# Eight token transfers per chunk of a recurrence, begun by GpSimd on its own queue instead of by SyncE

## The reference, cut to what matters

```python
x_proj = x @ W_in
xs, z = jnp.split(x_proj, 2, axis=-1)
delta = xs @ W_delta
Bv = xs @ W_B
Cv = xs @ W_C
deltaA = jnp.exp(jnp.einsum('bld,dn->bldn', delta, A))
deltaB = jnp.einsum('bld,bln->bldn', delta, Bv)

def step(state, inp):
    dA_i, dB_i, x_i, C_i = inp
    state = dA_i * state + dB_i * x_i[:, None, :]
    y = jnp.einsum('bdn,bn->bd', state, C_i)
    return (state, y)
```

## Time and profile before

| | before |
|---|---|
| median of three runs | 7372.27 us (7366.63 to 7378.81) |
| the profiled execution: its time / span | 7362.99 us / 7361.1 us |
| mean granted TensorE clock | 0.970 |
| recurrence, first to last scan | 2277.07 to 7018 us |
| VectorE busy | 6478.1 us (88%) |
| TensorE busy | 6408.9 us (87%) |
| GpSimd busy | 2747.4 us (37%) |
| transfers of tokens | 2048 of 16 KB and 128 of 4 KB, all issued by SyncE |

### The profile page before, as it was taken

The page is one execution under the profiler, slowest core; times in us unless marked ns, Lnnn a source line. Parts: engine busy times, 40 slices in busy tenths (PEclk is TensorE's granted clock), DMA queues, the critical chain, the costliest instruction groups (busy, mean ns, idle before and its releaser), DMA issues. The chain is left out here.

```text
span 7361.1 us, 173597 instructions
## 1 busy us (share of the span) xinstructions
PE 6408.9 (87%) x52385; PEld 3911.8 (53%) x52385; DVE 6478.1 (88%) x4166; ACT 4524.9 (61%) x9561; POOL 2747.4 (37%) x1996
## 2 busy tenths in 40 slices
PE   8999999999786888888888888888888888888867
PEld 3555547555344555555555555555555555555535
DVE  7888878888557999999999999999999999999962
ACT  7888868888464555555555555555555555555541
POOL 5555445555234333333333333333333333333300
PEclk9999999999898999999999999999999999999985
DMA  6666666666693111111111111111111111111154
GB/s 144 153 156 154 155 144 155 154 154 155 199 321 83 27 27 27 28 27 27 28 26 27 28 27 28 27 27 28 27 26 28 26 29 27 27 27 28 27 171 113
DMA packets 918664, 569.20 MB, mean 77 GB/s; under 512 B 710606, under 2 KB 819054, under 8 KB 917870
## 3 DMA queue, kind: packets, MB, share of 16 engines
q1 hardware_dynamic: 917885, 560.17, 32.1%
HBM read 161.99 MB, written 125.17 MB: 39 GB/s over the span
## 5 line engine op out<-in xcount | busy, mean ns | idle before, releaser
L1059 DVE TENSOR_TENSOR_SCAN states<-decay,enter_ps 128x1024 f32<-128x1024 f32 x2048 | 4468.2, 2262 | 172.3 <-ACT enter_ps L965 167.2
L876 PE MATMUL enter_ps<-s_steps,s_tokens 128*128 128x128 bf16 (+1 forms) x16384 | 2139.3, 311 | 625.6 <-DVE states L1059 514.5
L876 PEld LDWEIGHTS enter_ps<-s_steps,s_tokens 128*128 128x128 bf16 (+1 forms) x16384 | 1596.2, 130 | 1738.5 <-DVE states L1059 1569.4
L950 ACT ACTIVATE decay<-rate_ps 128x504 f32<-128x504 f32 x4096 | 2196.3, 588 | 98.0 <-PE rate_ps L854 23.8
L1016 POOL TENSOR_SCALAR s_wide<-s_rates,mask 128x512 bf16<-128x512 bf16 (+1 forms) x1088 | 1619.5, 1506 | 488.3 <-DMA s_rates<-rates_dram 353.8
L965 ACT COPY enter_ps<-states 128x16 f32<-128x16 f32 x1920 | 363.1, 189 | 1655.4 <-PE enter_ps L876 1649.6
L854 PE MATMUL rate_ps<-s_wide,s_decays 128*128 128x256 bf16 x8192 | 1330.9, 285 | 34.4 <-POOL s_wide L1016 33.7
L243 POOL TENSOR_TENSOR entered<-gates 128x512 f32<-128x512 f32 x512 | 900.9, 1760 | 888.8 <-ACT gates L203 888.8
L900 PE MATMUL y_ps<-states,spread 128*32 128x512 f32 x8320 | 1117.9, 609 | 0.4 <-issue 0.4
L1022 POOL COPY spread<-s_readout 128x64 f32<-128x64 f32 (+1 forms) x272 | 63.6, 234 | 2565.4 <-PE y_ps L900 2009.9
L854 PEld LDWEIGHTS rate_ps<-s_wide,s_decays 128*128 128x128 bf16 x8192 | 897.5, 119 | 95.8 <-issue 36.8
(11 more groups left out here) (154 smaller groups left out, 2310.4 us busy)
## 6 DMA issues: line engine op xcount, KB each, us to landing
rows<-feat SPq DMA_DIRECT2D x1024, 132.0 KB, 2.4
rows<-feat SPq DMA_DIRECT2D x512, 128.0 KB, 2.4
s_steps<-steps_dram SPq DMA_DIRECT2D x4096, 8.0 KB
rows<-feat SPq DMA_DIRECT2D x512, 127.8 KB, 2.4
s_rates<-rates_dram SPq DMA_DIRECT2D x256, 128.0 KB, 2.6
s_tokens<-tokens_dram SPq DMA_DIRECT2D x2048, 16.0 KB
rates_dram<-parts SPq DMA_DIRECT2D x32, 768.0 KB, 4.6
steps_dram<-steps SPq DMA_DIRECT2D x32, 768.0 KB, 8.0
```

Of the source, the lines that this page charges most:

```text
L876: mm = pe.matmul(out.rearrange("p h l -> p l h"), tokens[s][0:n * TERMS, k, :], steps[s][0:n * TERMS, k, 0:n, d:d + half], start=True, sto ...
L950: act.activation(decay[i][:, HEADS // 2 * h:HEADS // 2 * (h + 1), 1:], rate_ps[h][:, :, 0:n], ACT.Exp).then_inc(decay_ready, 1)
L1059: dve.tensor_tensor_scan(out, factor, term, 0.0, ALU.mult, ALU.add).then_inc(scanned, 1)
```

## The change

The eight transfers of tokens go from SyncE's `load` to GpSimd's `chunk`, between the widening and the wait for the readout. With them goes a copy of the wait for `enter_ready`; SyncE keeps its own for the steps. The tokens get semaphores of their own (`tokens_in`), and TensorE waits for both kinds. Sizes, addresses and the number of transfers stay the same.

```diff
+        tokens_in = [ctx.enter_context(nc.semaphore(f"scan_tokens_in{s}")) for s in range(SETS)]
...
-        LOADS = BLOCK + TERMS
...
                 sp.wait_ge(enter_ready, units_to(b, before(c) + 1))
                 sp.sem_inc(passed, 1)
-                for e in range(TERMS):
-                    a = STATE * (e // SPLITS)
-                    src = tokens_dram[bass.ds(b, 1), t0:t0 + n, a:a + STATE].rearrange("b (k t) n -> (b t) k n", t=BLOCK)
-                    sp.dma_start(tokens[s][e::TERMS, :, :], src).then_inc(enter_in[s], DMA)
                 for t in range(BLOCK):
...
-                    pe.wait_ge(enter_in[s], SCAN0 + (turn_of(b, c) + 1) * LOADS * DMA)
+                    pe.wait_ge(enter_in[s], SCAN0 + (turn_of(b, c) + 1) * BLOCK * DMA)
+                    pe.wait_ge(tokens_in[s], (turn_of(b, c) + 1) * TERMS * DMA)
...
                 w.then_inc(widened[s], 1)
+                pool.wait_ge(enter_ready, units_to(b, before(c) + 1))
+                pool.sem_inc(passed, 1)
+                for e in range(TERMS):
+                    a = STATE * (e // SPLITS)
+                    src = tokens_dram[bass.ds(b, 1), FULL * c:FULL * c + n, a:a + STATE].rearrange(
+                        "b (k t) n -> (b t) k n", t=BLOCK)
+                    pool.dma_start(tokens[s][e::TERMS, :, :], src).then_inc(tokens_in[s], DMA)
                 pool.wait_ge(readout_in[s], SCAN0 + (turn + 1) * DMA)
```

## The result

| | before | after |
|---|---|---|
| median (runs) | 7375.54 us (four, 7366.63 to 7379.01) | 7266.84 us (four, 7257.00 to 7271.46) |
| profiled execution: time / span | 7362.99 / 7361.1 us | 7257.00 / 7255.2 us |
| mean granted TensorE clock | 0.970 | 0.975 |

The ratio of the times is 0.9853, 95% interval 0.9836 to 0.9870: **faster by 1.5%, some 109 us**. The forecast was 7330 with a range from 7275 to 7510. The direction was right, the size was not.

The account below looks back on a forecast made before the run. Bound by VectorE's scans, and 14 times by SyncE's issuing. Holes -79 and -4, late chunk 0' +35 and first chunk +6 sum to -42 us: 7321 profiled, 7330 us on the median, range 7275 to 7510.

Parts of the forecast that it names:

- SyncE's issuing bounds the recurrence at 3': Before chunk 3 of the next batch, 14 times, scans wait for steps that SyncE issues 6 us late.
- 79 and 4 us of holes: VectorE's idle time before chunk 3' and right behind (79), and before chunks 1' and 2' (4); all predicted to go.
- the three loads 1', 2', 3': SyncE's loads between a batch end and the late steps; relieving them gives 16 us against a lateness of 6.
- The price x: GpSimd's time for one token transfer, taken as 1.0 us; the forecast sum is zero at 1.17.
- the chain: GpSimd's serial work at the batch end: eight issues, spread, loop end, widening, eight issues, landing; on time up to 0.86 us each.
- the +35: Chunk 0', first of the next batch, late 15 times by 16 - 13.7 us at 1.0 us per transfer.
- the formula: Chunk 0' late by 16x - 13.7 us, 15 times; first chunk later by 8x - 1.8; x is GpSimd's time per transfer.
- First chunk, +6: Before the very first scan: eight token issues on GpSimd make it 8 - 1.8 us later.
- The 17 us of second holes left: Second and third holes behind chunk 0' in some batches, 17 us in all, predicted to stay.
- The rival that counted them (7277): GpSimd nearly as quick as SyncE, x up to 0.86, second holes gone too: 7277 us; chance 0.22.
- Inside the batch nothing changes, and VectorE does not lock GpSimd out: Within a batch, 15.9 of 17.46 us needed, cost 0; rival of VectorE locking out GpSimd: 11500 us, chance 0.02.
- A draw or slower, 0.42 together: Draw: 0' takes what 3' gives, 7372 us, chance 0.13. Slower: GpSimd's serial chain bounds, 7505 to some 8400, chance 0.29.

Follow-up runs that it names:

- The runs with three chunks each: The change, but GpSimd begins tokens only of chunks 1, 2, 3 (0.9888), 15, 16, 0 (0.9859) or 8, 9, 10 (0.9992); ratios to the kernel before.
- the tokens on ScalarE one unit sooner: Kernel before with tokens begun by ScalarE, two transfers in unit 0, one in units 1 to 6, none in unit 7: 0.9896 of the kernel before.
- the run with chunks 1, 2, 3: The change with GpSimd beginning the tokens only of chunks 1, 2 and 3 of each batch, SyncE the others: 0.9888 of the kernel before.
- doubled: The change with every token transfer issued a second time by GpSimd, into a spare tile: 7321.54 us, 0.9928 of the kernel before.
- tripled: The change with two extra token transfers by GpSimd for each, 24 issues per chunk: 7766 us, 1.0536 of the kernel before.

## Why the prediction was wrong where it was

1. *SyncE's issuing bounds the recurrence at 3'; taking eight issues off each load ends that.* Right: I had added up 79 and 4 us of holes in the trace of before, and all of them went (79.3 and 3.8). The runs with three chunks each bear it out: relief near the batch end works, relief in mid-batch doesn't. The view that it takes the three loads 1', 2', 3' was right but too narrow. Relief ahead of 0' does as much.

2. ***The price x*: the step that failed.** I took 1.0 us and bounded it by 0.69 from below and 1.8 from above. The chip shows 0.51, half the forecast's value and below the lower bound. Two faults lie in it. The upper bound carried over a ratio from elementwise work (1760 against 678 ns) to an instruction that moves no elements. And the lower bound, SyncE's 0.69, held 0.13 us of register work between two issues; on GpSimd eight issues follow one another in 4.1 us with no gap between them. Even the 0.557 us of SyncE's instruction alone is more than GpSimd's 0.508. A bound "from below" that is another engine's price is no bound. With 0.51 the chain gives 16 x 0.51 = 8.2 against 13.7: no lateness at 0', and the +35 vanish. The rest of the chain was sized too short, which did not matter here: the formula would leave 5.5 us to spare at 0', and the trace has 2.8. GpSimd stood 1.44 us ahead of the issues for chunk 16, where I had nothing, and 2.86 us at its loop's end for 1.8, and the landing takes 2.0 us for 1.5.

3. *First chunk, +6.* The same fault and nothing else. With x = 0.51 the formula gives 4.1 - 1.8 = +2.3; the hole grew by 2.5.

4. *The 17 us of second holes left, because "they hang on the restart of TensorE after a pause".* Wrong in its conclusion, and the second fault in size. I had read the last link of the chain and not its first. The trace of before had the row (TensorE's timeline, batch end at 3454 us):

```profile
3456.11 1.03 PE L876 MATMUL enter_ps<-s_steps,s_tokens 128*128 128x128 bf16 x8 [1.34 <-DMA s_steps<-steps_dram]
3456.94 0.64 PE L854 MATMUL rate_ps<-s_wide,s_decays 128*128 128x256 bf16 x4
3460.45 1.62 PE L876 MATMUL enter_ps<-s_steps,s_tokens 128*128 128x128 bf16 x8 [2.87 <-DVE states L1059]
```

TensorE waited for the steps of 0' first, and was slower after that. At the five batch ends of this trace where it waited 1.28 us or more for them, the two later holes add up to 15.7 of the 17.4 us. The lateness had a cause, and it was SyncE. These holes went with the change, stayed where only 1, 2, 3 were relieved, and came back where GpSimd was made late. The link that I did name is not empty, though: with the tokens on ScalarE one unit sooner, and at two batch ends of the run with chunks 1, 2, 3 (0.99 and 1.65 us), third holes stand behind terms of 0' that were in time, at a granted clock of 0.72 in the 6 us from the first scan on. The rival that counted them (7277) was 10 us above the measured median.

5. *Inside the batch nothing changes, and VectorE does not lock GpSimd out.* Right. Eight issues took 4.25 us before the first scan and 4.06 to 4.19 amid scans. The Trainium skill (*SBUF — State Buffer*, Who interferes with whom) says that a VectorE instruction with at most one input in SBUF, outside the two-port modes, does not contend with GpSimd. These scans read the decays from SBUF and the entering terms from PSUM, and the trace shows no lock for them.

6. *A draw or slower, 0.42 together.* The mechanism was sound, as the doubled and tripled runs show. Its condition, x from 1.12 up, was far from met. The forecast's weight on it came from bounds that rested on no row of a GpSimd issue.

The Trainium skill (*DMA: Bandwidth & Descriptors*, Issuing engines are not separate DMA queues) says that issuing from several engines saves only sequencer time, "usually small relative to the DMA itself". That only sequencer time is saved agrees with the trace: the bytes are the same, and so is the DMA share of the recurrence (0.14 in the stretch of the earlier trace rows, before and after). For one transfer the issue is the smaller part, 0.51 us on GpSimd for 2.0 us to landing. But what is small for one transfer is not small in sum: on SyncE the issues filled 16.4 of 17.46 us, and moving eight of them was worth 109 us, 1.5%.

## What to carry to other kernels

The engine that begins DMAs has no busy share on the page; add up its issues over one period of the loop and compare the sum with the period, then look for the place where it is late for the first time. Relief paid only between the last place where it was ahead and the tight place, and three chunks in seventeen gave here as much as all of them. A wait at a loop's turn can hide from the next instruction and appear one or two steps later, so follow a hole back to the first late transfer before calling it fixed. Where the price of an instruction isn't in the trace and the forecast turns on it, say that other engines' prices are no bounds, and keep the rival on the cheap side heavy.

## What the hardware showed that I had not expected

- GpSimd begins a 16 KB token transfer in 0.51 us, less than SyncE's 0.557 with the register work on top, and a steps transfer in 0.547, twice SyncE's 0.278. SyncE's price differs by a factor of two between these two shapes, GpSimd's by 8%. Why, I have not tried.
- A transfer begun by ScalarE (0.56 us) runs beside ScalarE's own activations and costs them nothing that shows: they take 588 ns on average with it and without it.
- After a pause of 2 to 4 us around a late start, TensorE's granted clock was 0.72 or 0.53 on average over the following 6 to 8 us, a mixture of its two levels of 1.2 and 2.4 GHz, where the batch without a late start stayed at 1.00 (4593 to 4601 us). Eight matmuls took 1.50 to 1.86 us instead of 1.03. A late start ahead of TensorE's loop turn is paid again in the units behind it: on average over the 13 turns, 2.0 us late cost 3.7 in holes, and 4.1 late cost 6.4.
